# Film factors computed as rows of conditions, bias rows spread in one accumulated product, a new order of pieces: two conditioned attention layers on one core

## The chip, the cores and the metric

The kernel runs on one core of one Trainium2 chip. The metric is the device time of one execution in microseconds (us); lower is better. The core has five engines that run their own instruction streams: TensorE (PE; its weight loads are listed apart as PEld), VectorE (DVE), ScalarE (ACT), GpSimd (POOL) and SyncE (SP), which here only issues DMAs. They wait for each other through semaphores.

## The reference

For 32 sequences of 256 tokens with 256 features, two layers are computed one after the other (masks are all one here, but the kernel handles them):

```python
# layer 0: 8 heads of 32; softmax over features (q) and over time (k)
xn = ln(x, ln_w, ln_b)
q = softmax((xn @ Wq + bq) per head, axis=features)
k = softmax((xn @ Wk + bk + mask) per head, axis=time)
v = (xn @ Wv + bv) * mask
att = einsum('bnhd,bnhl->bhdl', k, v);  y = einsum('bnhd,bhdl->bnhl', q, att)
scale, shift = split(silu(emb) @ W_emb + b_emb)      # emb: 32 x 512, W_emb: 512 x 512
x = x + silu(ln(y) * (1 + scale) + shift) @ W_out + b_out
# layer 1: 16 heads of 16; ordinary attention over 256 tokens, softmax over keys
q, k, v = (xn @ q_w + q_b), (xn @ k_w + k_b), (xn @ v_w + v_b) * mask
y = softmax(q k^T + mask) v;  then the same film, silu and output product as above
```

`silu(emb) @ W_emb` is the film product: it is made once for each layer and for all 32 sequences.

## The kernel before, in words

One "batch" b is one sequence. The work on it is cut into pieces with names: `s0(b)` (statistics of x on VectorE), `r0(b)` (their reciprocal root on GpSimd), `z0(b)` (normalised x, as a high and a low half in f16), `k0`, `q0`, `v0` (projections on TensorE), `km`, `ke`, `kt`, `rk` (softmax of k), `qm`, `qs`, `qe`, `rq` (softmax of q), `att`, `y0`, `Y0(b)` (attention and its division), `s1`, `r1`, `yn0`, `y0T`, `th0`, `st0`, `sh0`, `sl0` (norm, film and silu), `o0`, `x1(b)` (output product and the sum with x: the end of layer 0). Layer 1 has `s2`, `z1`, `q1p`, `k1p`, `v1p`, `qa`, `ka`, `spq`, `spk` (high and low halves of q and k), `rows(b,u)` (scores, for the maximum), `max_(b,u)` on VectorE, `cols(b,u)` (transposed scores), `exp(b,u)` on ScalarE, `pv(b,u)`, `Y1_`, `y1T`, `th1`, `o1` and `o(b)`.

Each engine's stream is a list of such calls written out by hand, in which pieces of some six batches are interleaved, and each piece waits on the semaphores of those that it needs. Where a product lands among the eight PSUM banks is a table, `BANK`, and what must have been read from that bank before is a second table, `FREED`. SP's stream is such a list too: `x_in(b)` loads x, `z0T` and `z1T` transpose by DMA, `wq(b)`/`wk(b)` write the halves of q and k to DRAM and `rq6(b)`/`rk6(b)` read them back in the layout of `rows`.

Ahead of batch 0 stands a setup, whose pieces have no batch number. Weights are loaded (`ld_w1`, `ld_w0`), their largest entries are found and made into powers of two (`w0m`, `w1m`, `mx_w0`, `mx_w1`, `w0p`, `w1p`; TensorE's `tr_*` and `ar_*` carry the maxima across partitions), and each weight is split into f16 halves (`wh_*` on ScalarE at L1739, `wl_*` on VectorE at L1345). Four bias rows are products of a norm's bias with a weight: `row0` to `row3` (L930). To three of them VectorE adds the layer's own bias (`fr0`, `fr1`, `fr2`, L1357), a product with ones spreads the sum over all partitions (`bb0` to `bb2`, L937), and ScalarE copies it out (`bc0` to `bc2`, L1760). Layer 1's q and k biases are needed as columns with the features in another order: ScalarE's `perm` permutes the two biases (L1751) and the two weights (L1754), and `col` multiplies (L990, L991). The film products are `fm0` and `fm1` (L973): for each of four blocks of 128 outputs and each of four blocks of 128 inputs, a 128 x 128 block of the f32 film weight is loaded as the stationary operand and the 32 conditions (`csT`) stream past. `f0m` and `f1m` make the film factors from them on VectorE. `fill_*` (L1775) writes constants into the score operands on ScalarE.

A f32 product stands in the trace as two records, each with its own weight load; a transpose or a f16 product as one.

## Time and profile before

| what | value |
|---|---|
| time before, median of 3 runs | 878.3 us (876.21 to 880.64) |
| profiled execution, its own time | 878.06 us |
| its span, first to last instruction | 876.2 us |
| busy: PE, DVE, POOL, ACT | 827.4, 792.1, 725.7, 708.0 us |

The profiled execution took 878.06 us, of which 1.9 us lie outside the span. Busy time is the time in which at least one instruction of an engine was running. Starts in the rows below are in us from the beginning of the span.

### The profile page before, as it was taken

What the parts mean: (1) busy time and instruction counts of PE and PEld (TensorE: products, weight loads), DVE (VectorE), ACT (ScalarE), POOL (GpSimd) and SP (SyncE); (2) the same over time, 40 slices, a digit from 0 to 9 for tenths busy, and PEclk for the clock granted to TensorE, in tenths of its full rate; (3) what the DMA queues carried; (4) which work ended last, traced back from release to release, by engine and by line L of the source; (5) the groups of instructions that cost most, each with busy time, mean ns of one, the idle gap of its engine ahead of it and who ended that gap; (6) DMA issues with size and microseconds to landing.
All of it is one profiled execution on the core that took longest, in us unless ns stands there. A gap on an engine that the chain in (4) does not pass through costs nothing.

```text
span 876.2 us, 25220 instructions
## 1 busy us (share of the span) xinstructions
PE 827.4 (94%) x8651; PEld 603.3 (69%) x8651; DVE 792.1 (90%) x1633; ACT 708.0 (81%) x1253; POOL 725.7 (83%) x1205
## 2 busy tenths in 40 slices
...
GB/s 230 68 38 33 117 98 92 106 102 109 49 126 133 98 91 115 91 116 110 81 129 57 137 91 102 96 108 116 118 109 89 74 114 91 95 126 113 74 43 37
DMA packets 149306, 85.84 MB, mean 98 GB/s; under 512 B 87478, under 2 KB 141852, under 8 KB 149180
## 3 DMA queue, kind: packets, MB, share of 16 engines
...
## 4 chain that ended last, share of the span: by engine, by line
PE 39%; POOL 19%; DVE 14%; issue 11%; ACT 5%; DMA 0%; SPq 0%; POOLq 0%; DVEq 0%; ACTq 0%
PE banks L688 11%; PE banks L835 7%; DVE NM L1247 4%; PE banks L696 4%; PE banks L822 4%; PE banks L811 4%; POOL ZHL L1928 3%; PE banks L703 3%; POOL Z L1921 3%; DVE st L1148 2%; PE banks L845 2%; POOL YN L1912 2%; POOL SH L1966 2%; POOL ZHL L1925 2%; POOL AB L1994 2%
## 5 line engine op out<-in xcount | busy, mean ns | idle before, releaser
L1247 DVE TENSOR_REDUCE NM<-banks 128x4 f32<-128x1024 f32 x256 | 302.6, 1212 | 12.2 <-PE banks L811 11.6
L1714 ACT ACTIVATE wraw<-banks,uu 128x1024 f32<-128x1024 f32 x154 | 170.2, 1136 | 22.0 <-PE banks L822 21.4
L1714 ACT ACTIVATE PX<-banks,uu 128x1024 f32<-128x1024 f32 x102 | 112.9, 1138 | 11.4 <-PE banks L822 9.9
L688 PE MATMUL banks<-wo,SH 128*128 128x256 f16 x768 | 96.7, 278 | 5.2 <-POOL SH L1966 4.3
L1908 POOL TENSOR_TENSOR rs<-ve,nhalf 128x2 f32<-128x2 f32 x128 | 91.0, 711 | 10.6
L688 PE MATMUL banks<-wv,ZT 128*128 128x256 f16 x768 | 98.6, 280 | 0.9 <-DVE NM L1247 0.8
L811 PE MATMUL banks<-SK,SQ 51*128 51x256 f16 x1024 | 89.3, 273 | 8.0 <-DVE NM L1247 3.9
L1966 POOL TENSOR_TENSOR SH<-ST,SH 128x512 f16<-128x512 f32 x64 | 73.8, 1158 | 26.1 <-ACT SH L1682 26.1
L1696 ACT ACTIVATE R<-banks,fcs,sqs 128x256 f32<-128x256 f32 x128 | 73.5, 574 | 26.7 <-PE banks L696 20.3
L822 PE MATMUL banks<-SQ,SK 53*128 53x256 f16 x1024 | 90.0, 272 | 5.0 <-ACT wemb L1722 1.3
L1928 POOL TENSOR_TENSOR ZHL<-Z,ZHL 128x256 f16<-128x256 f32 x128 | 87.8, 706 | 5.3
L688 PEld LDWEIGHTS banks<-wo,SH 128*128 128x128 f16 x768 | 73.4, 99 | 23.1 <-POOL SH L1966 9.1
L688 PEld LDWEIGHTS banks<-wv,ZT 128*128 128x128 f16 x768 | 74.8, 100 | 17.3 <-issue 7.5
L835 PE MATMUL banks<-wraw,V 128*32 128x256 f32 x1232 | 85.1, 385 | 1.6 <-ACT wraw L1714 0.6
L1994 POOL TENSOR_TENSOR AB<-R,AB 128x512 f16<-128x512 f32 x64 | 74.5, 1166 | 6.0 <-ACT AB L1696 5.7
L1669 ACT ACTIVATE TH<-banks,hB,hA 128x256 f32<-128x256 f32 x128 | 66.2, 580 | 15.7 <-PE banks L703 14.2
L1921 POOL TENSOR_SCALAR Z<-X,nm,rs 128x256 f32<-128x256 f32 x128 | 74.5, 588 | 3.6 <-POOL ZHL L1928 0.5
L1912 POOL TENSOR_SCALAR YN<-Y,nm,rs 128x256 f32<-128x256 f32 x128 | 72.7, 575 | 2.5
L1696 ACT ACTIVATE AB<-banks,fcs,sqs 128x256 f16<-128x256 f32 x128 | 74.0, 578 | 0.0
L811 PEld LDWEIGHTS banks<-SK,SQ 51*128 51x128 f16 x1024 | 39.1, 94 | 47.6 <-issue 25.3
L822 PEld LDWEIGHTS banks<-SQ,SK 53*128 53x128 f16 x1024 | 38.1, 94 | 45.8 <-issue 27.2
L1906 POOL TENSOR_SCALAR nm<-mv 128x2 f32<-128x2 f32 x128 | 29.0, 226 | 49.0 <-DVE mv L1151 48.2
...
## 6 DMA issues: line engine op xcount, KB each, us to landing
...
```

Of the source, the lines that this page charges most:

```text
L688: m = PE.matmul(dst[:, t, :], zt[:, j, k, t * P:(t + 1) * P], w[:, i, k, :], start=(k, n) == (0, 0), stop=(k, n) == (1, 2))
L811: m = PE.matmul(banks[:, n + j % 2, (j // 2) * T:(j // 2) * T + T], SQ[p, r, h, c * P:(c + 1) * P], SK[p, r, h, :], start=True, stop=True)
L822: m = PE.matmul(banks[:, n + j % 2, (j // 2) * T:(j // 2) * T + T], SK[p, r, h, c * P:(c + 1) * P], SQ[p, r, h, :], start=True, stop=True)
L835: m = PE.matmul(banks[32 * j:32 * j + 32, n, 0:T], V1[:, r, c, 4 * g + j, :], px((8 * b + u) % 5)[:, at_px(j):at_px(j) + T], start=(c == 0 ...
L1247: V.tensor_reduce(NMe[:, c, :, 2 * g:2 * g + 2], banks[:, n:n + 2, :].rearrange("p a (h m) -> p a h m", m=T), AX.X, ALU.max, negate=True). ...
L1696: t = A.activation(dst, bank(home(f"g{c}1", b))[:, f, :], ACT.Identity, bias=fcs[:, i, f:f + 1], scale=sqs[:, i:i + 1])
L1714: A.activation(px(v % 5), banks[:, n:n + 2, :].rearrange("p a n -> p (a n)"), ACT.Exp, scale=uu[:, 0:1]).then_inc(S["exp"])
L1908: G.tensor_tensor(rs[:, b % 2, l, :], ve[:, l, :], nhalf[:, :], ALU.pow).then_inc(S[f"r{l}"])
L1921: i = G.tensor_scalar(Z[:, t, :], src[:, t, :], nm[:, b % 2, 2 * l, t:t + 1], rs[:, b % 2, 2 * l, t:t + 1], ALU.add, ALU.mult)
L1928: i = G.tensor_tensor(h[:, 1, k], z[:, :, k, :], h[:, 0, k], ALU.subtract)
L1966: G.tensor_tensor(SH[:, l, 1], ST[:, l], SH[:, l, 0], ALU.subtract).then_inc(S[f"sl{l}"])
L1994: G.tensor_tensor(AB[:, i, :, 1], R1[:, i], AB[:, i, :, 0], ALU.subtract).then_inc(S["sp" + c])
```

## The change

Five things change; the loops, the arithmetic on each batch and all DMA sizes stay.

1. Film: the conditions become the stationary operand (32 columns) and the film weight streams past them, 512 columns at a time (`fx0`, `fx1`, 4 products each). ScalarE copies the 32 x 512 result into the film weight's own tile (`fy0`, `fy1`), and `fm0`/`fm1` are now four transposes of 32 x 128 each.
2. `bb0` to `bb2` take the product with the weight (the norm's bias broadcast over 128 columns) and the layer's bias row in one accumulation; `row0` to `row2` and `fr0` to `fr2` are gone.
3. `rw` makes layer 1's q and k bias rows complete (6 products); `perm` permutes these two rows alone, and `col` is four products of one column.
4. The four copies of weights in `perm` are gone, and with them `xb1(0)`'s wait for `col`.
5. All streams, banks and `FREED` entries are in a new order, SP's too. Counted in pieces, up to `x1(0)` VectorE's list lacks `fr0`, `fr1`, `fr2`, `o1m`, `mx_o1`, `km(3)` and `at_(2)`, and has nothing that stood behind it before.

```diff
-            def bias_all(i):
-                ready(e, f"fr{i}", "cst")
-                clear(e, f"gbb{i}", 0)
-                PE.matmul(at_all(i), ones3[0:1, :], frow[:, i, :], start=True, stop=True).then_inc(C["PE"])
+            def bias_all(i, l, w):
+
+                e.wait_ge(l_w[l], 80)
+                e.wait_ge(l_row, 96)
+                ready(e, "cst")
+                clear(e, f"gbb{i}", 0)
                 for k in range(2):
+                    PE.matmul(at_all(i), lnc[:, l, 1, k:k + 1].to_broadcast([P, P]), wraw[:, 3 * l + w, k, :],
+                              start=(k == 0), stop=False)
+                PE.matmul(at_all(i), ones3[0:1, :], brow[:, i, :], start=False, stop=True).then_inc(C["PE"])
...
-            def film(l):
+            def cond_rows(l):
+
                 ready(e, "csT")
                 e.wait_ge(l_f[l], 64)
+                clear(e, f"gfx{l}", 0)
+                for k in range(4):
+                    t = PE.matmul(at_conds(l), csT[:, k, :], wemb[l][:, k, :], start=(k == 0), stop=(k == 3))
+                t.then_inc(C["PE"])
+
+            def film(l):
+                ready(e, f"fy{l}", "cst")
                 clear(e, f"gfm{l}", 0)
                 for m in range(4):
-                    for k in range(4):
-                        t = PE.matmul(at_film(l, m), wemb[l][:, k, m * P:(m + 1) * P], csT[:, k, :],
-                                      start=(k == 0), stop=(k == 3))
+                    t = PE.transpose(at_film(l, m), wemb[l][0:NB, 0, m * P:(m + 1) * P], ident[0:NB, 0:NB])
                 t.then_inc(C["PE"])
...
+            def rw():
+
+                e.wait_ge(l_w[1], 80)
+                e.wait_ge(l_row, 96)
...
+                for i in range(2):
+                    for k in range(2):
+                        PE.matmul(at_rows(i), lnc[:, 1, 1, k:k + 1], wraw[:, 3 + i, k, :], start=(k == 0), stop=False)
+                    t = PE.matmul(at_rows(i), one1[0:1, 0:1], brow1[:, i, :], start=False, stop=True)
...
-            def bias_sum(i):
-                ready(e, f"row{i}")
-                e.wait_ge(l_row, 96)
-                V.tensor_tensor(frow[:, i, :], at_row(i)[0:1, :], brow[:, i, :], ALU.add).then_inc(C["DVE"])
...
             def perm():
...
-                    for k, e0 in ((0, 0), (0, 1), (1, 0), (1, 1)):
-                        t = A.activation(XB1[:, i, k, e0 * P:(e0 + 1) * P].rearrange("p (f h) -> p f h", f=16),
-                                         wraw[:, 3 + i, k, :].rearrange("p (h e f) -> p e f h", e=2, f=16)[:, e0], ACT.Identity)
...
-            ld_m(); ld_c(); x_in(0); x_in(1); ld_w1(); x_in(2); ld_w0(); mbd0(); ld_r(); ld_f1(); ld_o1(); am(0)
+            ld_m(); ld_c(); x_in(0); x_in(1); ld_w1(); x_in(2); ld_w0(); ld_r(); mbd0(); ld_o0(); ld_f1(); am(0)
```

**TensorE, the setup.** The first place is TensorE's stream from the conditions' transposes to the first projection; each row is an instruction, its output and operands, and how often it follows itself. Before (`row2`, `row1`, ... , the film products, then `k0(0)`):

```order
L964 MATMUL banks<-ident,SQ 128x32 x4
L922 MATMUL banks<-ident,SK 128x32 x4
L930 MATMUL banks<-wraw,lnc 1x256 x4
L865 MATMUL banks<-ident,mxw 3x128
L930 MATMUL banks<-wraw,lnc 1x256 x4
L937 MATMUL banks<-SQ,ones 128x256
L865 MATMUL banks<-ident,mxw 3x128
L937 MATMUL banks<-SQ,ones 128x256
L973 MATMUL banks<-csT,wemb 128x32 x32
L718 MATMUL banks<-ZT,wk 128x256 x6
```

and of the change, from `ar_w0` to the first projections (`rw`, `fx1`, `tr_o0`, `fx0`, `bb0`, `v0(0)`, `v0(1)`, `fm0`, `q0(0)`, `q0(1)`):

```order
L870 MATMUL banks<-mxd,ones 128x3
L995 MATMUL banks<-wraw,lnc 1x256 x2
L996 MATMUL banks<-SK,one 1x256
L995 MATMUL banks<-wraw,lnc 1x256 x2
L996 MATMUL banks<-SK,one 1x256
L965 MATMUL banks<-wemb,csT 32x512 x4
L864 MATMUL banks<-ident,mxw 1x128
L965 MATMUL banks<-wemb,csT 32x512 x4
L939 MATMUL banks<-wraw,lnc 128x256 x2
L941 MATMUL banks<-SK,ones 128x256
L687 MATMUL banks<-wv,ZT 128x256 x24
L972 MATMUL banks<-ident,wemb 128x32 x4
```

The 32 film products with 32 columns became 8 with 512; `row0` to `row2` left, `rw` came, and `v0` and `q0` of batches 0 and 1 now stand ahead of `k0(0)`, with the film transposes between them.

**VectorE, ahead of the first `V`.** The second place is what VectorE does just before the first value tile `v(0)` (L1189 before, L1202 now). Before:

```order
L1345 SCALAR_TENSOR_TENSOR wq<-wraw,sl,wq 128x256 x2
L1148 BN_STATS st<-X 128x6 x2
L1151 BN_AGGR mv<-st 128x2 x2
L1345 SCALAR_TENSOR_TENSOR wk<-wraw,sl,wk 128x128 x4
L1288 TENSOR_REDUCE mxc<-banks 1x1
L1289 TENSOR_SCALAR mxd<-ident,mxc 1x1
L1162 TENSOR_REDUCE km<-banks 128x2
L1163 TENSOR_SCALAR km<-km,un 128x2
L1345 SCALAR_TENSOR_TENSOR wv<-wraw,sl,wv 128x256 x2
L1189 SCALAR_TENSOR_TENSOR V<-banks,un,bbc 128x512
```

and of the change:

```order
L1458 CAST p<-SQ 1x256
L1358 SCALAR_TENSOR_TENSOR wv<-wraw,sl,wv 128x256 x4
L1301 TENSOR_REDUCE mxc<-banks 1x1
L1302 TENSOR_SCALAR mxd<-ident,mxc 1x1
L1358 SCALAR_TENSOR_TENSOR wk<-wraw,sl,wk 128x256 x2
L1358 SCALAR_TENSOR_TENSOR wq<-wraw,sl,wq 128x256 x2
L1202 SCALAR_TENSOR_TENSOR V<-banks,un,bbc 128x512
L1161 BN_STATS st<-X 128x6 x2
L1164 BN_AGGR mv<-st 128x2 x2
```

`s0(3)`, `s0(4)`, `f0m`, `f1m`, `km(0)`, layer 1's `wl_q1` and `wl_k1` and `o1m` moved from ahead of `v(0)` to behind it.

**SP, the first score operands.** The third place is SP's queue around `rk6(0)`, the loads of batch 0's k halves. Before (`wq(0)`, `z1T(1)`, `rq6(0)`, `wk(0)`, `x_in(6)`, `x_in(7)`, `rk6(0)`):

```order
L541 DMA scr<-AB 128x4x256
L521 DMA_TRANSPOSE ZT<-ZHL 128x8x128
L554 DMA SQ<-scr 32x2048
L555 DMA SQ<-scr 16x2048
L554 DMA SQ<-scr 32x2048
L555 DMA SQ<-scr 16x2048
L541 DMA scr<-AB 128x4x256
L514 DMA X<-in_x_dram 128x2x256 x2
L554 DMA SK<-scr 32x2048
```

and of the change (`z1T(0)`, `z0T(5)`, `z1T(1)`, `wq(0)`, `wk(0)`, `mbd1`, `x_in(6)`, `rq6(0)`, `rk6(0)`):

```order
L520 DMA_TRANSPOSE ZT<-ZHL 128x8x128 x3
L540 DMA scr<-AB 128x4x256 x2
L641 DMA mhd<-mh 32x3x256
L513 DMA X<-in_x_dram 128x2x256
L553 DMA SQ<-scr 32x2048
L554 DMA SQ<-scr 16x2048
L553 DMA SQ<-scr 32x2048
L554 DMA SQ<-scr 16x2048
L553 DMA SK<-scr 32x2048
```

`x_in(7)` moved behind `rk6(0)`, and `wq(0)` behind `z1T(1)`. On ScalarE, one `fill` (`fill_q0`) moved from ahead of the `wh_*` to just ahead of `wh_k1` and `ke(0)`.

## Rows read from the trace of the kernel before

**Rows 1.** The page: busy time by engine, share of the span, instructions

```profile
PE 827.4 (94%) x8651; PEld 603.3 (69%) x8651; DVE 792.1 (90%) x1633; ACT 708.0 (81%) x1253; POOL 725.7 (83%) x1205
```

**Rows 2.** Stages: start:end and length, busy (count) of engines, clock, DMA

```profile
10.40:44.40 34.00, 32.52 (x153) 25.15 (x152) 31.63 (x105) 27.87 (x36) 20.40 (x35) 0.70 0.47 129
44.40:70.25 25.85, 25.14 (x210) 21.94 (x209) 23.79 (x67) 11.90 (x28) 16.63 (x27) 0.94 0.16 32
70.25:111.65 41.40, 33.47 (x267) 28.18 (x265) 34.68 (x107) 23.25 (x54) 36.32 (x59) 0.92 0.35 86
150.00:850.00 700.00, 684.51 (x7576) 492.26 (x7572) 652.06 (x1256) 602.41 (x1067) 600.45 (x988) 1.00 0.41 101
```

**Rows 3.** Timeline of VectorE: start, length, instruction

```profile
13.91 0.41 DVE L1357 TENSOR_TENSOR SQ<-banks,SK 1x256 f32<-1x256 f32 x1
...
44.48 0.74 DVE L1189 SCALAR_TENSOR_TENSOR V<-banks,un,bbc 128x512 f32<-128x512 f32 x1
...
70.25 0.74 DVE L1227 SCALAR_TENSOR_TENSOR X<-banks,un,XB 128x512 f32<-128x512 f32 x1
...
111.65 3.48 DVE L1247 TENSOR_REDUCE NM<-banks 128x4 f32<-128x1024 f32 x3
```

**Rows 4.** The same timeline: the work that moves behind `v(0)`

```profile
24.29 1.44 DVE L1345 SCALAR_TENSOR_TENSOR wq<-wraw,sl,wq 128x128 f16<-128x128 f32 x4
...
32.43 0.15 DVE L1383 TENSOR_SCALAR be1c<-bec 128x2 f32<-128x2 f32 x1
...
38.18 0.16 DVE L1399 SCALAR_TENSOR_TENSOR mxw<-bnd 128x1 f32<-128x1 f32 x1
...
39.20 0.74 DVE L1148 BATCH_NORM_STATS2 st<-X 128x6 f32<-128x256 f32 x2
...
40.14 1.72 DVE L1345 SCALAR_TENSOR_TENSOR wk<-wraw,sl,wk 128x128 f16<-128x128 f32 x4
...
42.22 0.67 DVE L1162 TENSOR_REDUCE km<-banks 128x2 f32<-128x512 f32 x1
```

**Rows 5.** Timeline of TensorE (matmuls) in the setup

```profile
15.10 2.79 PE L930 MATMUL banks<-wraw,lnc 128*1 128x256 f32 x8
...
20.05 13.59 PE L973 MATMUL banks<-csT,wemb 128*128 128x32 f32 x64
...
42.39 2.73 PE L688 MATMUL banks<-wq,ZT 128*128 128x256 f16 x12
...
48.84 1.47 PE L688 MATMUL banks<-wq,ZT 128*128 128x256 f16 x12
```

**Rows 6.** TensorE's weight loads around the first change of pace

```profile
16.34 0.13 PEld L930 LDWEIGHTS banks<-wraw,lnc 128*1 128x1 f32 x1 [0.30 <-issue]
16.77 0.13 PEld L930 LDWEIGHTS banks<-wraw,lnc 128*1 128x1 f32 x1 [0.30 <-issue]
17.08 0.30 PEld L930 LDWEIGHTS banks<-wraw,lnc 128*1 128x1 f32 x2 [0.19 <-issue]
```

**Rows 7.** Granted clock (third from the end) by stretches, columns as in Rows 2

```profile
19.00:20.00 1.00, 1.00 (x8) 0.91 (x6) 0.80 (x5) 1.00 (x1) 0.92 (x3) 1.00 0.92 327
...
24.00:28.00 4.00, 4.00 (x21) 4.00 (x20) 3.96 (x8) 4.00 (x12) 2.15 (x2) 0.50 0.03 9
80.00:90.00 10.00, 9.23 (x65) 7.54 (x64) 8.34 (x28) 4.50 (x10) 7.55 (x15) 0.74 0.28 51
```

**Rows 8.** Timeline of ScalarE in the setup

```profile
15.85 5.30 ACT L1775 ACTIVATE SK<-one 32x6144 f16<-32x6144 f32 x1
...
43.18 0.56 ACT L1640 ACTIVATE KE<-banks,km,un 128x256 f32<-128x256 f32 x1 [4.88 <-DVE km L1163]
```

**Rows 9.** SP's queue ahead of the first scores

```profile
99.01 3.12 SPq L514 DMA_DIRECT2D X<-in_x_dram  x2
102.42 0.33 SPq L554 DMA_DIRECT2D SK<-scr  x1
```

**Rows 10.** TensorE's gap between 74 and 79 us, and what ended it

```profile
78.11 0.88 PE L703 MATMUL banks<-ident,KE 128*128 128x128 f32 x4 [3.24 <-ACT KE L1640]
```

More of the change, by code:

```diff
@@ L88 @@
+    "gt_o1": "5",
+    "ga_o1": "2",
+    "gt_f0": "2",
+    "ga_f0": "3",
+    "gt_f1": "0",
+    "ga_f1": "0",
+    "gt_b": "5",
+    "ga_b": "2",
+    "gfx0": "6",
     "gfm0": "1",
+    "gfx1": "1",
     "gfm1": "5",
@@ L258 @@
     "PE": (
-        "cnd pm row2 row1 tr_w1 row0 row3 bb2 tr_w0 bb1 ar_w1 bb0 ar_w0 fm1 fm0 tr_o0 col tr_f0 ar_o0 ar_f0 "
-        "tr_o1 tr_f1 ar_o1 tr_b ar_b ar_f1 ").split(),
+        "pm cnd bb2 tr_w1 row3 tr_w0 ar_w1 bb1 ar_w0 rw fx1 tr_o0 fx0 bb0 fm0 fm1 col tr_f0 ar_o0 ar_f0 tr_b "
+        "tr_o1 ar_b tr_f1 ar_o1 ar_f1 ").split(),
     "DVE": (
-        "mb0 csl csT w1m fr2 fr1 w0m mx_w1 fr0 mc mx_w0 w1p w0p o1m wl_q1 p3 wl_v0 wl_k0 o0m f1m f0m wl_q0 "
-        "wl_k1 mx_o0 wl_v1 mx_f0 o0p film0 mx_o1 wl_o0 bm mx_b o1p mx_f1 fcs mb1 film1 wl_o1 ").split(),
+        "mb0 csl mc csT w1m w0m mx_w1 mx_w0 w1p w0p o0m p3 wl_v1 wl_v0 mx_o0 wl_k0 wl_q0 f0m f1m mx_f0 o0p "
+        "wl_q1 wl_k1 film0 wl_o0 bm mx_b o1m mx_o1 fcs mb1 o1p mx_f1 film1 wl_o1 ").split(),
     "ACT": (
-        "th fill_k1 fill_q0 fill_k0 wh_q1 wh_k1 wh_q0 bc0 wh_v0 wh_k0 perm wh_v1 bc1 fill_q1 wh_o0 bc2 wh_o1 ").split(),
+        "th fill_k0 fill_k1 wh_v0 wh_v1 fy1 wh_q0 wh_q1 wh_k0 fy0 bc1 perm bc0 fill_q0 wh_k1 fill_q1 wh_o0 "
+        "bc2 wh_o1 ").split(),
     "POOL": (
@@ L987, in col @@
                     for f in range(2):
-                        o, cc = at_col(2 * i + f), slice(f * P, (f + 1) * P)
-                        for k in range(2):
-                            PE.matmul(o, XB1[:, i, k, cc], lnc[:, 1, 1, k:k + 1], start=(k == 0), stop=False)
-                        t = PE.matmul(o, prow[:, i, cc], one1[0:1, 0:1], start=False, stop=True)
+                        t = PE.matmul(at_col(2 * i + f), prow[:, i, f * P:(f + 1) * P], one1[0:1, 0:1], start=True, stop=True)
                 t.then_inc(C["PE"])
-            cnd_t(); pm(); row2(); row1(); tr_w1(); row0(); row3(); bb2(); tr_w0(); bb1(); ar_w1(); bb0(); ar_w0()
@@ L1005, in _ @@
-            pv(0, 3); cols(0, 5); k0(8); ty(0, 0); q0(8); v0(8); ktT(8); pv(0, 4); pv(0, 5); rows(2, 2)
-            rows(2, 3); att(7); q1p(4); rows(2, 4); k1p(4); rows(2, 5); rows(2, 6); cols(0, 6); o0(5); cols(0, 7)
+            pm(); cnd_t(); bb2(); tr_w1(); row3(); tr_w0(); ar_w1(); bb1(); ar_w0(); rw(); fx1(); tr_o0(); fx0()
+            bb0(); v0(0); v0(1); fm0(); q0(0); q0(1); fm1(); k0(0); col(); k0(1); ktT(0); tr_f0(); ar_o0(); v0(2)
+            att(0); qtT(0); q0(2); k0(2); k0(3); ktT(1); y0(0); q0(3); qtT(1); att(1); ar_f0(); y0(1); y0T(0)
```

928 lines of the change are left out of this document (460 added, 468 removed), and 214 rows, old and new, of the table FREED.

## The prediction

> **What bounds the kernel now.** I read the busy times first: TensorE 94% of the span, VectorE 90% [rows 1]. Then the stages. From 150 to 850 us TensorE is busy for 684.5 of 700 us and VectorE for 652.1 [rows 2]: two engines are nearly full at once, on work that this change doesn't touch. That part can be reordered but hardly shortened: TensorE's idle time in it, 15.5 us, is the most that another order could win there, while a bad order has no such limit. So an early start pays in full only if nothing later waits longer; and it is the first 111.65 us, up to VectorE's first `max_` [rows 3], that the change rewrites.
>
> In that beginning VectorE is the engine to watch. From 10.4 to 44.4 us it is busy for 31.63 of 34 us, from 44.4 to 70.25 (the first `x1`) for 23.79 of 25.85, and from there to the first `max_` for only 34.68 of 41.4 [rows 2, 3]: first its own queue is the limit, then a chain of latencies. TensorE looks as full in the setup, but 13.59 us of it are the film products [rows 5], and the projections queue behind them. VectorE doesn't wait for this, since its own list, with both films and layer 1's weights ahead of `v(0)`, is just as long: `v(0)` starts at 44.48 [rows 3].
>
> **The clock in the setup.** The weight loads of L930 (256 f32 columns a record) start 0.43 us apart at 16.34 and 16.77, and 0.31 us later comes a row that holds two loads in 0.30 us [rows 6]: the pace doubles at about 17 us, after some microseconds of such products without a gap (8 records from 15.10 on take 2.79 us [rows 5], where 0.43 each would be 3.4). So one record of 256 columns is 0.43 us at 1.2 GHz and 0.21 at 2.4 GHz; the f16 products show the same ratio (12 in 2.73 or 1.47 us, the drain of the last included [rows 5]). Under the film products the granted clock is 0.50, where it was 1.00 at 19 to 20 us [rows 7], and a film record takes 13.59/64 = 0.21 us although only 32 columns stream: the load of 128 f32 columns is what it waits for.
>
> **The change part by part.**
>
> *Film.* 64 records of 0.21 us go. 16 records of 512 columns come. The trace before has no 512-column f32 product; bounded by the nearest, it is between two records of 256 columns at full clock (0.43) and two at half (0.86), so 6.8 to 13.7 us for both layers. At half clock nothing is gained. I take full clock for nearly all of it, because the row with the longest gapless stretch of wide f32 columns, L930, is the one after which the pace doubled, while the film products, with 32 columns between loads, ran at 0.50 throughout [rows 5 to 7].
>
> A page speaks against any gain here: the Trainium skill, "TensorE: Matmul & The Clock Gate", section "LDWEIGHTS (loading the stationary operand)", gives the load's time as its columns divided by 1.2 GHz, whatever the array's clock. By that the 64 loads of the old form would be 6.8 us, as much as the new form's best case, and this term would be zero. The trace disagrees for f32: 0.21 us a record at half clock [rows 5], so the sum goes by the row.
>
> *Bias rows.* `row0` to `row2` and `bb0` to `bb2` become three products of six records each: on TensorE as many wide records as before (12 and 6). What goes is the three adds of VectorE, 0.41 us each (one row stands for the three [rows 3]), 1.2 us of a full queue, and the trip TensorE, VectorE, TensorE. In exchange `bb2` now needs the bias rows at once. VectorE's first add ran at 13.91, so they had landed by then, and they are now issued one DMA earlier. I let TensorE start there at 13.9; before, `row2`, 4 records, needed only the weights and ran ahead of this, so these records move later.
>
> *`rw`, `col`, `perm`.* `rw` adds 12 records of 256 columns (2.6 to 5.1 us), `col` shrinks to four one-column products, and ScalarE loses eight permuting copies. ScalarE isn't the limit: it waited 4.88 us ahead of its first `ke` [rows 8]. It does get one `fill` of 5.3 us [rows 8] between the weights and `ke(0)`, which used to lie in its early idle time. `km(0)` is itself later in VectorE's list than the fill's end, so I cost it at nothing; uncovered it would be 5.3 us on `ke(0)`, though VectorE has `s0(4)`, `f1m` and `q1(1)` to do before it needs ScalarE's results. The 32 x 512 copies and the transposes of 32 rows are in no row; I bound them by zero and the 0.74 us of a 128 x 512 operation, and the waiting engine has other work.
>
> *When TensorE reaches `v0(0)`.* `bb2` (6 records) and `row3` (4) at half clock take 4.3 us from 13.9, to 18.2; the maxima and `bb1` follow, with waits for VectorE, until about 20. Then `rw` 12, `fx1` and `fx0` 16 of double width, `bb0` 6: 50 units of 256 columns. At 0.21 us that ends at 30.7, at 0.43 us at 41.4. `v0(0)` adds 1.3 or 2.7: done at 32.0 or 44.1. A relapse to half clock of some 3 us would cost 1.7.
>
> *When VectorE reaches `v(0)`.* Before: 44.48. Out of its way go `f1m`, `s0(3)` and `f0m` (32.43 to 38.3, 5.8 us), `s0(4)` and `wl_k1` (39.20 to 41.8, 2.6), `wl_q1` 1.4, `km(0)` 0.9, `o1m` 0.7 (as the reduction of 512 columns) and the adds 1.2 [rows 3, 4]: 12.6 us, so it is ready at 31.9. TensorE is done at 32.0 to 33.7; `v(0)` starts at about 33.
>
> *From there to `x1(0)`.* VectorE was busy for 23.8 us between the two [rows 2]. Added is the moved work without the adds, 11.4; gone from ahead of `x1(0)` are `at_(2)`, `km(3)`, `mx_o1` and `o1m`, together 2.7: 32.5 us. Without any idle time `x1(0)` starts at 65.5; with 1.5 us of idle time, where it had 2.1, at 67, 3.3 us before its 70.25.
>
> *From `x1(0)` to the scores.* SP's two loads of x held its queue for 3.12 us from 99.01, and only then, at 102.42, came `rk6(0)` [rows 9]. `x_in(7)`, the one that waits for GpSimd's `xb0(4)`, is now behind it. At most 3.4 us; but `wq(0)` now stands behind `z1T(1)`, and `rq6(0)` waits for that write. I take 1.0 of it. What queued behind `x_in(7)` is only batch 7's load, which has 20 us.
>
> *Sum.* 3.3 + 1.0 = 4.3 us off the profiled execution's span of 876.2, 871.9; with the 1.9 us outside it 873.8. The median of the runs, 878.3, is 0.2 above the profiled execution's 878.06, so the two bases agree.
>
> **The rivals.**
>
> *The lead is swallowed.* From 150 us on the engines work in a fixed order, and any wait for a bank or an SP entry in the new order eats the lead. For it: POOL is busy for 36.3 of the 41.4 us before the first `max_` [rows 2], and its work there is not shorter. Against it: later both full engines have 15.5 and 48 us of slack in 700. Half to all of the lead gone gives 876 to 878.
>
> *The clock stays low (slower than before).* If the wide f32 products are not enough for 2.4 GHz, or the gaps at `tr_w0`, `ar_w1` and `ar_w0` undo it, TensorE ends `v0(0)` at 44.1, VectorE stands idle from 31.9 on, and `x1(0)` comes no sooner than 44.1 + 32.5 = 76.6, 6.4 us late: 883.5 with the 1.0 from SP. It decides from the point at which `v0(0)` ends later than 70.25 - 32.5 = 37.8. Against it stand L930's rows.
>
> *The new order is itself better or worse in the full part.* 15.5 us of TensorE idle time can shrink or double. A third of it either way is 5 us: 869 or 879, and 884 for a bad one.
>
> *The luck of a gap.* Before, TensorE stood 3.24 us for `ktT(4)` [rows 10], and the mean clock of the next 10 us was 0.74 [rows 7], so some 2.6 us of work was lost on a stretch where VectorE also waits. `ktT(4)` now stands further back, behind layer 1's first products. If no such gap opens, the first `max_` is 2 us earlier still: 871.8.
>
> **How the numbers follow.** The forecast (a lead of 2.5 to 9 us that is kept) has 0.50, the last rival inside it; of this 0.43 is beyond 0.5%, 4.4 us, which is about what a measurement of this kernel can tell from no change. The swallowed lead has 0.26, all of it within 0.5%. The low clock has 0.12, slower. The reordered full part has 0.12: 0.04 faster, 0.08 slower. Together faster 0.47, same 0.33, slower 0.20. The predicted time is the likeliest's, 873.8. The range reaches down to 868.5 (`v(0)` at 32.0, no idle time before `x1(0)`, the whole of SP's 3.4 us: 5.7 + 3.4 = 9.1) and up to 882.5, which takes in the swallowed lead and the milder losses of order, and leaves out the low clock and a bad order.
>
> **What would show it.** Right: the 512-column records of `fx1` and `fx0` about 0.43 us apart and granted clock 1.00 over most of 21 to 31 us; `v0(0)` ended by 34; VectorE's first `V` at 33 and first `X` (L1227's successor) at 66 to 68; the first `max_` at 106 to 108; TensorE busy for 97 to 98% from 150 to 845 us. Wrong: 0.86 us between those records; a VectorE gap ahead of `V` or `km`; the first `max_` early and the end not, which puts the loss into the full part.

## The result and the profile after

The changed kernel takes 885.12 us (median of 20 runs, 883.56 to 887.77), the kernel before 879.11 us on the same chip (20 runs, 876.21 to 883.88). The ratio is 1.0065, 95% interval 1.005 to 1.0079: slower, outside the forecast's range. The profiled execution took 884.83 us, 883.0 of them in the span; before, 876.2.

The page's busy times of the changed kernel, which answer to [rows 1]:

```profile
PE 825.6 (94%) x8607; PEld 587.0 (66%) x8607; DVE 795.9 (90%) x1630; ACT 706.4 (80%) x1247; POOL 727.1 (82%) x1205
```

Every engine has about as much work as before, TensorE 1.8 us less, and the span is 6.8 us longer: something waits. The stages, cut at the same events as [rows 2] (the first `V`, the first `X`, the first `max_`):

```profile
10.40:41.31 30.91, 27.73 (x72) 10.29 (x73) 16.66 (x53) 13.81 (x21) 12.74 (x20) 1.00 0.53 135
...
20.40:33.00 12.60, 12.60 (x26) 3.55 (x25) 8.49 (x32) 1.70 (x4) 3.05 (x7) 1.00 0.72 166
...
41.31:76.60 35.29, 28.93 (x235) 24.05 (x233) 32.61 (x106) 24.55 (x38) 23.62 (x41) 0.96 0.13 24
76.60:116.00 39.40, 32.22 (x269) 27.62 (x267) 36.45 (x115) 21.96 (x51) 36.93 (x60) 0.98 0.41 100
150.00:850.00 700.00, 680.41 (x7516) 487.20 (x7514) 660.27 (x1259) 596.71 (x1056) 601.89 (x985) 1.00 0.43 100
```

In the first stage VectorE works for 16.66 of 30.91 us, where it was the full engine before (31.63 of 34). Its timeline names what it waited for:

```profile
34.60 0.28 DVE L1301 TENSOR_REDUCE mxc<-banks 1x1 f32<-1x128 f32 x1 [4.92 <-PE banks L864]
...
38.30 0.88 DVE L1358 SCALAR_TENSOR_TENSOR wk<-wraw,sl,wk 128x256 f16<-128x256 f32 x2 [3.18 <-ACT wk L1738]
...
41.31 0.75 DVE L1202 SCALAR_TENSOR_TENSOR V<-banks,un,bbc 128x512 f32<-128x512 f32 x1 [1.34 <-issue]
...
76.60 0.75 DVE L1240 SCALAR_TENSOR_TENSOR X<-banks,un,XB 128x512 f32<-128x512 f32 x1 [1.52 <-PE banks L687]
...
115.97 1.22 DVE L1260 TENSOR_REDUCE NM<-banks 128x4 f32<-128x1024 f32 x1
```

`v(0)` starts at 41.31, 3.2 us earlier than in [rows 3] but 8 later than forecast, and right behind `v0(0)`, the first 12 of the 24 records at L687, which start at 39.73 and take some 1.4 us. The view puts VectorE's last 1.34 us of idle time down to "issue", which names no other engine; by these times it was TensorE. `x1(0)` starts at 76.60, 6.4 late; the first `max_` at 115.97, 4.3 late; the last `o(31)` at 879.6, 6.8 late (before, 872.8). Both long waits come out of TensorE's queue: `tr_o0` (L864) stands behind `fx1`, and ScalarE's copy `fy1`, which waits for `fx1`, stands ahead of the cast of `wk`. TensorE's timeline (L939 with L941 is `bb2` at 13.58 and `bb1` at 19.62, L929 `row3`, L995 `rw`, L965 `fx1` and then `fx0`, L687 `v0(0)` with `v0(1)`):

```profile
13.58 2.04 PE L939 MATMUL banks<-wraw,lnc 128*128 128x256 f32 x4 [6.13 <-DMA SK<-in_L_cond_k_b_dram]
15.56 1.22 PE L941 MATMUL banks<-SK,ones 1*128 1x256 f32 x2
...
17.01 1.86 PE L929 MATMUL banks<-wraw,lnc 128*1 128x256 f32 x4
...
19.62 2.08 PE L939 MATMUL banks<-wraw,lnc 128*128 128x256 f32 x4
...
23.00 1.86 PE L995 MATMUL banks<-wraw,lnc 128*1 128x256 f32 x4
...
28.46 5.90 PE L965 MATMUL banks<-wemb,csT 128*32 128x512 f32 x8
...
34.49 3.62 PE L965 MATMUL banks<-wemb,csT 128*32 128x512 f32 x8
...
39.73 2.79 PE L687 MATMUL banks<-wv,ZT 128*128 128x256 f16 x24
```

TensorE stands still for 6.13 us until the bias rows are there. From 13.58 on it works without a gap, but at half pace: four records of 256 columns take 1.86 to 2.08 us throughout, and `fx0`, with the same eight records as `fx1`, needs 3.62 where `fx1` needed 5.90. The weight loads inside `fx1` show the change:

```profile
31.87 0.18 PEld L965 LDWEIGHTS banks<-wemb,csT 128*32 128x32 f32 x1 [0.68 <-issue]
32.73 0.18 PEld L965 LDWEIGHTS banks<-wemb,csT 128*32 128x32 f32 x1 [0.68 <-issue]
33.34 0.11 PEld L965 LDWEIGHTS banks<-wemb,csT 128*32 128x32 f32 x1 [0.44 <-issue]
```

0.86 us a record, then less from 33.1 on. So 1.2 GHz until 33.1 us. The clock column of the stage 20.40 to 33.00 says 1.00 all the same: the trace's clock records begin at 33.09, and the view takes a stretch ahead of the first record as full. Ahead of it, only the pace of like instructions tells the clock; "granted clock 1.00 over most of 21 to 31 us", which the forecast named as a sign of being right, can be read off this view and means nothing there.

SP's queue, as in [rows 9], with the first of `rk6(0)` at the second row:

```profile
103.01 0.38 SPq L513 DMA_DIRECT2D X<-in_x_dram  x1
...
105.70 0.30 SPq L553 DMA_DIRECT2D SK<-scr  x1
```

`rk6(0)` comes 29.1 us behind `x1(0)` (before 32.2), and the first `max_` 39.4 us behind it (before 41.4).

### The profile page after: what moved, and what is told of

It is laid out like the page before. It is cut to its first block, busy times and chain, and to the rows that moved or that the text cites. A ratio compares the mean times of both kernels' runs of the same rounds, so it can differ in the third digit from the quotient of the medians.

```text
span 883.0 us, 25115 instructions
## 1 busy us (share of the span) xinstructions
PE 825.6 (94%) x8607; PEld 587.0 (66%) x8607; DVE 795.9 (90%) x1630; ACT 706.4 (80%) x1247; POOL 727.1 (82%) x1205
## 4 chain that ended last, share of the span: by engine, by line
PE 40%; DVE 25%; POOL 15%; issue 12%; ACT 5%; SPq 1%; DMA 1%; POOLq 0%; DVEq 0%; ACTq 0%
PE banks L687 9%; DVE NM L1260 9%; PE banks L834 7%; PE banks L695 5%; PE banks L821 4%; PE banks L810 3%; DVE st L1161 3%; PE banks L702 2%; PE banks L844 2%; POOL ZHL L1934 2%; POOL Z L1927 2%; POOL SH L1972 2%; PE banks L753 2%; DVE ST L1229 1%; POOL XB L1993 1%
## 5 line engine op out<-in xcount | busy, mean ns | idle before, releaser
L687 PE MATMUL banks<-wo,SH 128*128 128x256 f16 x768 | 97.8, 280 | 9.6 <-POOL SH L1972 9.1
L1972 POOL TENSOR_TENSOR SH<-ST,SH 128x512 f16<-128x512 f32 x64 | 73.9, 1163 | 26.8 <-ACT SH L1681 26.7
L687 PE MATMUL banks<-wv,ZT 128*128 128x256 f16 x768 | 94.4, 273 | 1.6 <-DVE X L1240 1.0
L687 PEld LDWEIGHTS banks<-wo,SH 128*128 128x128 f16 x768 | 73.6, 100 | 28.1 <-POOL SH L1972 12.2
L687 PEld LDWEIGHTS banks<-wv,ZT 128*128 128x128 f16 x768 | 72.8, 98 | 15.2 <-issue 7.3
L1918 POOL TENSOR_SCALAR YN<-Y,nm,rs 128x256 f32<-128x256 f32 x128 | 74.7, 590 | 2.8
```

The costliest lines, as they stand in the source:

```text
L687: m = PE.matmul(dst[:, t, :], zt[:, j, k, t * P:(t + 1) * P], w[:, i, k, :], start=(k, n) == (0, 0), stop=(k, n) == (1, 2))
L1972: G.tensor_tensor(SH[:, l, 1], ST[:, l], SH[:, l, 0], ALU.subtract).then_inc(S[f"sl{l}"])
```

## The experiments

Theory L: the loss is TensorE's late `v0(0)`, at 1.2 GHz behind an idle gap. Rivals: the new order of the full part costs it, wherever the start is (O); the content, that is what is computed and how, costs in any order (C); the setup lists of VectorE and ScalarE cost it (Q). Theory M, for the clock itself: it comes up once wide products stand together. All ratios are to the kernel before, run on the same chip.

| kernel | ratio | 95% interval | `v(0)` | `x1(0)` | last `o(31)` |
|---|---|---|---|---|---|
| changed | 1.0065 | 1.005 to 1.0079 | 41.3 | 76.6 | 879.6 |
| + dummies in the gap | 0.9974 | 0.996 to 0.9988 | 32.2 | 66.3 | 868.5 |
| `rw` first | 1.0006 | 0.999 to 1.0022 | 38.9 | 73.0 | 875.0 |
| `rw` first + dummies | 0.9991 | 0.9969 to 1.0012 | 33.8 | 68.0 | 873.2 |
| `row3` ahead of `tr_w1` | 1.007 | 1.0052 to 1.0088 | 42.1 | 76.1 | 878.3 |
| without VectorE's two waits | 1.0071 | 1.0046 to 1.0095 | 41.2 | 76.5 | 879.6 |
| old order, film, transposes late | 1.0093 | 1.0072 to 1.0114 | 50.3 | 76.3 | 877.7 |
| old order, film | 1.0007 | 0.9991 to 1.0022 | 43.8 | 69.5 | 870.3 |
| old order, all, transposes late | 1.0075 | 1.0041 to 1.0109 | 49.4 | 74.9 | 874.5 |
| the same + dummies | 1.0073 | 1.0054 to 1.0092 | 49.6 | 74.3 | 879.5 |
| old order, all | 1.0027 | 0.9997 to 1.0057 | 53.3 | 79.1 | 879.7 |
| old order, all + dummies | 0.9972 | 0.9955 to 0.999 | 43.4 | 68.7 | 870.9 |
| before + dummies | 0.9999 | 0.9977 to 1.002 | 43.9 | 70.7 | 874.9 |

The starts are those of each profiled execution; before, they are 44.5, 70.2 and 872.8.

**Work in the gap.**

```diff
+            def warm(k):
+                for i in range(k):
+                    PE.matmul(banks[0:32, 7, :].rearrange("p (a n) -> p a n", a=4), ident[:, 0:32],
+                              ident[:, :].unsqueeze(1).to_broadcast([P, 4, P]), start=True, stop=True)
...
-            pm(); cnd_t(); bb2(); tr_w1(); row3(); tr_w0(); ar_w1(); bb1(); ar_w0(); rw(); fx1(); tr_o0(); fx0()
+            pm(); cnd_t(); warm(4); bb2(); tr_w1(); row3(); tr_w0(); ar_w1(); bb1(); ar_w0(); rw(); fx1(); tr_o0(); fx0()
```

> The changed kernel with four dummy f32 products of 512 columns added on TensorE between the transposes of the conditions and bb2 (weights and moving data are the identity, the output goes to bank 7, which nobody has used yet), in the 6.1 us in which TensorE otherwise waits for the bias rows. Nothing else moves. Theory L (low clock): the late v0(0) is the price of 1.2 GHz from 13.6 to 33.1 us; then with work in the gap the clock is full well before 28 us, the 8 records of fx1 take about 3.5 us in place of 5.9, v0(0) starts at 31 to 34 in place of 39.7, v(0) at 33 to 37 in place of 41.3, x1(0) at 67 to 71 in place of 76.6, and the time falls by 5 to 8 us against the changed kernel, 0.998 to 1.001 of the kernel before. Theory O (the new order of the full part costs the time, wherever the start is): v0(0) may come earlier, but the ratio stays at 1.005 or above. Mixed: x1(0) as early as before and still 2 to 4 us lost by the end, ratio about 1.003.

Measured: 0.9974. Three weight loads of the dummies, then TensorE and VectorE of this kernel:

```profile
10.78 0.18 PEld L1009 LDWEIGHTS banks<-ident 128*32 128x32 f32 x1 [0.68 <-issue]
11.63 0.12 PEld L1009 LDWEIGHTS banks<-ident 128*32 128x32 f32 x1 [0.68 <-issue]
12.07 0.11 PEld L1009 LDWEIGHTS banks<-ident 128*32 128x32 f32 x1 [0.32 <-issue]
```

```profile
7.36 5.72 PE L1009 MATMUL banks<-ident 128*32 128x512 f32 x8
13.28 1.10 PE L939 MATMUL banks<-wraw,lnc 128*128 128x256 f32 x4 [0.19 <-issue]
...
21.67 3.62 PE L965 MATMUL banks<-wemb,csT 128*32 128x512 f32 x8
...
25.42 3.62 PE L965 MATMUL banks<-wemb,csT 128*32 128x512 f32 x8
```

```profile
32.23 0.75 DVE L1207 SCALAR_TENSOR_TENSOR V<-banks,un,bbc 128x512 f32<-128x512 f32 x1 [1.32 <-issue]
...
66.31 0.75 DVE L1245 SCALAR_TENSOR_TENSOR X<-banks,un,XB 128x512 f32<-128x512 f32 x1 [0.36 <-PE banks L687]
...
105.59 1.22 DVE L1265 TENSOR_REDUCE NM<-banks 128x4 f32<-128x1024 f32 x1
```

The pace doubles at 11.6 us, inside the dummies; the same four records of `bb2` take 1.10 us instead of 2.04, `fx1` 3.62 instead of 5.90. `x1(0)` comes 10.3 us earlier than in the changed kernel, and the last `o(31)` 11.1 earlier: what is won at the start stays, and the work and order of all engines are otherwise the same. So the loss is TensorE at 1.2 GHz, and O can't explain more than a small part. That the idle gap is why the clock stays low, the other half of theory L, is not shown by this: the dummies fill the gap, but they are also products of another shape. `v(0)` waits for TensorE here too: VectorE's `wl_q0` ends at 30.91, and `v0(0)` only starts at 30.66. The expectation of the second run below takes VectorE's list for the limit, which is not so.

**Moving real work into the gap, without and with dummies.** `rw` goes ahead of `bb2`, its products with the bias rows last, its two rows in two banks; `k0(1)` then has to wait for `perm`.

```diff
-        at_rows = lambda i: banks[0:1, home("grw"), i * D:(i + 1) * D]
+        at_rows = lambda i: banks[0:1, (home("grw"), 7)[i], 0:D]
...
-            pm(); cnd_t(); bb2(); tr_w1(); row3(); tr_w0(); ar_w1(); bb1(); ar_w0(); rw(); fx1(); tr_o0(); fx0()
+            pm(); cnd_t(); rw(); bb2(); tr_w1(); row3(); tr_w0(); ar_w1(); bb1(); ar_w0(); fx1(); tr_o0(); fx0()
```

> The changed kernel with rw moved from behind ar_w0 to the front, ahead of bb2: its eight records with layer 1's weights need no bias row and can run from 9.65 us on, where the kernel before ran row2 and row1; only its four records with the bias rows wait for the DMA of 13.5 us. The two rows go to two banks (5 and 7) in place of one, and k0(1) waits for perm. No work is added. Theory L (what was lost is TensorE's time at 1.2 GHz after an idle gap): even if the clock stays at half as long as in the changed kernel, 3.7 us of work have left the stretch behind 13.6 us, so v0(0) starts at about 36 in place of 39.7 and x1(0) at 73, ratio about 1.002; if the work in the gap also brings the clock up, as the dummies did, v0(0) starts at 29 to 31, VectorE is the limit, x1(0) at 66 to 67 and the ratio is 0.996 to 0.999. If neither, above 1.004, the dummies helped for another reason.

> rw at the front and two of the dummy products (four records, 2.9 us) ahead of it, in the 2.4 us in which TensorE waits for layer 1's weights. Theory L: the clock comes up at about 12 us as with the four dummies, and 3.2 us of rw are out of the way behind 13.6 us, so v0(0) could start at 28. VectorE's list is the limit then, it was ready for v(0) at 31.2 with the four dummies: x1(0) at 66 and the ratio 0.996 to 0.999, the same as with the four dummies alone. It would be markedly better only if VectorE's list were not the limit, and it would be at 1.001 or above if the clock stays low again.

TensorE with `rw` first, without dummies:

```profile
9.82 3.57 PE L994 MATMUL banks<-wraw,lnc 128*1 128x256 f32 x8 [2.40 <-DMA lnc<-in_L_cond_norm_b_dram]
14.24 1.86 PE L997 MATMUL banks<-SK,one 1*1 1x256 f32 x4 [0.84 <-DMA SK<-in_L_cond_k_b_dram]
...
25.47 6.46 PE L965 MATMUL banks<-wemb,csT 128*32 128x512 f32 x8
...
37.30 2.79 PE L687 MATMUL banks<-wv,ZT 128*128 128x256 f16 x24
```

In this execution the clock stayed low until 31.2 us, but `v0(0)` starts 2.4 us earlier than in the changed kernel (36 was foreseen), and `x1(0)` is at 73.0, as worked out for this case. The ratio is 1.0006. So the late queue and the low clock both count, and real work in the gap did not bring the clock up in this execution: f32 products ran from 9.82 us on, with one pause of 0.84 us. That speaks against the idle gap as the whole reason. (One of its 12 runs took 874.62 us, 2.9 less than the next; whether its clock came up early is not known.) With two dummies ahead of `rw` the clock rises at 12.5, and then a new gap appears:

```profile
21.60 5.29 PE L965 MATMUL banks<-wemb,csT 128*32 128x512 f32 x8 [1.92 <-DVE iu L1351]
...
27.02 3.62 PE L965 MATMUL banks<-wemb,csT 128*32 128x512 f32 x8
```

```profile
22.80:26.10 3.30, 3.30 (x5) 0.69 (x4) 3.11 (x13) 1.70 (x4) 1.02 (x3) 0.50 1.18 233
```

TensorE is early now, but waits 1.92 us for the bank that VectorE's `w1p` frees, so `fx1` starts at 21.60, where it started at 21.67 with the dummies alone: the work moved ahead wins nothing. At 22.8, 1.2 us after that gap, the granted clock falls to 0.50, `fx1` takes 5.29 us in place of 3.62, and `x1(0)` is 1.7 us later than with the dummies alone. The ratio, 0.9991, is just above what was expected.

**Other neighbours, the same work.**

```diff
-            pm(); cnd_t(); bb2(); tr_w1(); row3(); tr_w0(); ar_w1(); bb1(); ar_w0(); rw(); fx1(); tr_o0(); fx0()
+            pm(); cnd_t(); bb2(); row3(); tr_w1(); tr_w0(); ar_w1(); bb1(); ar_w0(); rw(); fx1(); tr_o0(); fx0()
```

> The changed kernel with row3 and tr_w1 exchanged on TensorE: the four wide records of row3 follow bb2 at once, and the small transpose comes behind both. The work is the same. Theory M (what decides is whether wide products stand together, not how long TensorE has been busy): 10 wide records in a row bring the clock up by some 20 us instead of 33, v0(0) starts at 31 to 34, less the 1.9 us by which tr_w1 and so VectorE's scales are late, x1(0) at 68 to 70, ratio 0.998 to 1.001. If only a busy stretch without a gap counts, or chance of alignment, the exchange changes nothing: v0(0) at about 40, ratio 1.005 to 1.009.

Measured: 1.007. The ten wide records run from 12.41 to 17.3 us without a gap, and the clock still comes up only at 34.5. Theory M falls for this case. `v0(0)` starts at 40.5.

**VectorE's two waits taken away.**

```diff
-            p3_(); wl_v1(); wl_v0(); mx_o0(); wl_k0(); wl_q0(); v(0); s0(3); f0m(); q1(0); v(1); qm(0); km(0)
+            p3_(); wl_v1(); wl_v0(); wl_k0(); wl_q0(); mx_o0(); v(0); s0(3); f0m(); q1(0); v(1); qm(0); km(0)
...
-            th(); fill_k0(); fill_k1(); wh_v0(); wh_v1(); fy1(); wh_q0(); wh_q1(); wh_k0(); fy0(); bc1(); perm()
+            th(); fill_k0(); fill_k1(); wh_v0(); wh_v1(); wh_k0(); wh_q0(); fy1(); wh_q1(); fy0(); bc1(); perm()
```

> The changed kernel with VectorE's two longest waits ahead of v(0) taken away: mx_o0 (4.92 us for tr_o0 behind fx1) goes behind wl_k0 and wl_q0, and ScalarE casts wk and wq of layer 0 ahead of its copy fy1 (3.18 us for wk). TensorE's work and order stay. Theory L: these waits lay under TensorE's late v0(0), so VectorE only waits longer ahead of v(0), which stays at 40.5 to 41.5; x1(0) 75.5 to 76.6 and the ratio 1.004 to 1.008. Rival Q (the new order of VectorE's and ScalarE's setup lists is what costs): x1(0) at 70 or earlier and the ratio below 1.002.

VectorE's waits between 10 and 70 us in this kernel (us in total, times, longest), and its `v(0)`:

```profile
DVE V L1202 <- PE banks L687: 6.2, 1, 6.2
DVE mxc L1301 <- PE banks L864: 6.2, 3, 3.3
```

```profile
41.22 0.75 DVE L1202 SCALAR_TENSOR_TENSOR V<-banks,un,bbc 128x512 f32<-128x512 f32 x1 [6.19 <-PE banks L687]
```

The wait for ScalarE's `wk` is gone and the rest has moved in front of `v(0)` itself: 6.19 us for `v0(0)`, with `v(0)` at the same place to 0.1 us and the ratio at 1.0071. The two waits that the profile of the changed kernel shows most plainly lay under TensorE's delay. Rival Q falls: with these two taken away nothing is won, and with the dummies the changed kernel's own lists give `v(0)` at 32.2.

**The film alone in the old order.**

```diff
-            fm1(); fm0(); k0(0); v0(0); tr_o0(); col(); tr_f0(); q0(0); ar_o0(); v0(1); ar_f0(); tr_o1(); ktT(0)
+            fx1(); fx0(); k0(0); v0(0); fm1(); fm0(); tr_o0(); col(); tr_f0(); q0(0); ar_o0(); v0(1); ar_f0(); tr_o1(); ktT(0)
```

> The kernel before with the film change alone, in its own order: fx1 and fx0 stand where the 64 film products stood, the transposes fm1 and fm0 behind k0(0) and v0(0), and ScalarE's two copies behind wh_k0. Theory L: ahead of these products TensorE starts its setup at 9.65 us as before and is at half clock when it reaches them (24 us); 16 records cost 13.7 us at half clock, what the old form cost, or 6.9 at full. If the clock comes up as long as they run, they take 8 to 11 us, v0(0) is done earlier than before, VectorE's v(0) stays at 44.5 because VectorE's own list is as long, and the ratio is 0.997 to 1.002. If the content of this edit were itself the loss (transposes and ScalarE's copies as a chain), film0 and with it th0(0) would be late and the ratio above 1.004.

Measured: 1.0093, a miss of my own making. Its TensorE, and VectorE's longest wait:

```profile
33.14 1.04 PE L723 MATMUL banks<-ZT,wk 128*128 128x256 f16 x6 [4.56 <-DMA augs<-p]
```

```profile
DVE be1c L1400 <- PE banks L985: 6.1, 1, 6.1
```

The transposes stood behind `k0(0)`, which waits 4.56 us for the DMA of `augs`, and VectorE's `f1m` waited for them. With them directly behind `fx0`:

```diff
-            fx1(); fx0(); k0(0); v0(0); fm1(); fm0(); tr_o0(); col(); tr_f0(); q0(0); ar_o0(); v0(1); ar_f0(); tr_o1(); ktT(0)
+            fx1(); fx0(); fm1(); fm0(); k0(0); v0(0); tr_o0(); col(); tr_f0(); q0(0); ar_o0(); v0(1); ar_f0(); tr_o1(); ktT(0)
```

> The film change alone in the old order once more, mended where the first try was slow by its own doing: there the transposes stood behind k0(0), which waits 4.6 us for the DMA of augs, and VectorE waited 6.1 us for them ahead of f1m. Now fm1 and fm0 follow fx0 at once. Nothing else differs from the kernel before than the film products and the two copies on ScalarE. Theory: fx1 and fx0 take 8.8 us as there, the transposes end at about 29.8, VectorE reaches f1m at 32.1 and does not wait, v(0) at 44 to 45, x1(0) at 69.5 to 71, ratio 0.998 to 1.002. If the film change itself costs, VectorE waits ahead of be1c again and the ratio is above 1.004.

Measured: 1.0007, `v(0)` at 43.8 and `x1(0)` at 69.5. Two short groups of transposes on the wrong side of one waiting product had cost 6.8 us at `x1(0)`. Put right, the film change costs and gives nothing in the old order.

**The whole change in the old order.** First with the transposes late, without and with four dummies (`warm(4)` behind `pm()`), then in the right place (`fm1(); fm0();` directly behind `fx0();`). The diffs of the first to the kernel before, TensorE's and ScalarE's and VectorE's lists; the functions are those of the change:

```diff
-            cnd_t(); pm(); row2(); row1(); tr_w1(); row0(); row3(); bb2(); tr_w0(); bb1(); ar_w1(); bb0(); ar_w0()
-            fm1(); fm0(); k0(0); v0(0); tr_o0(); col(); tr_f0(); q0(0); ar_o0(); v0(1); ar_f0(); tr_o1(); ktT(0)
+            cnd_t(); pm(); tr_w1(); row3(); bb2(); tr_w0(); bb1(); ar_w1(); bb0(); ar_w0()
+            rw(); fx1(); fx0(); k0(0); v0(0); fm1(); fm0(); tr_o0(); col(); tr_f0(); q0(0); ar_o0(); v0(1); ar_f0(); tr_o1(); ktT(0)
...
-            mb0(); csl_(); s0(0); s0(1); csT_(); s0(2); w1m(); fr2(); fr1(); w0m(); mx_w1(); fr0(); mc(); mx_w0()
+            mb0(); csl_(); s0(0); s0(1); csT_(); s0(2); w1m(); w0m(); mx_w1(); mc(); mx_w0()
...
-            th(); fill_k1(); fill_q0(); fill_k0(); wh_q1(); wh_k1(); wh_q0(); bc0(); wh_v0(); wh_k0(); perm()
+            th(); fill_k1(); fill_q0(); fill_k0(); wh_q1(); wh_k1(); wh_q0(); bc0(); wh_v0(); wh_k0(); fy1(); fy0(); perm()
```

> The content of the whole change (film past the conditions, three bias products, q and k biases of layer 1 as rows, no adds on VectorE) in the order of the kernel before on all engines, with its banks. What is left out is the new order alone. TensorE's first wide product still waits for the bias rows or for tr_w1, till 12 to 14 us. Theory L: clock at half till some 30 us, k0(0) and v0(0) end at 40 to 44; VectorE has its old long list, ready for v(0) at 43.3 (44.5 less the adds), so x1(0) at 69.5 to 71.5 and the ratio 0.998 to 1.002, well below the changed kernel. Theory C (the content is what costs, in any order): x1(0) later than 74, ratio above 1.004.

> The same as the content in the old order, with the four dummy products of 512 columns (identity by identity, into bank 7, which rw uses later) on TensorE behind its first transposes. Theory L: the clock comes up before fx1, k0(0) and v0(0) end by 35, VectorE never waits for them, x1(0) at 68.5 to 69.5, ratio 0.996 to 0.999, at most 1 us better than without the dummies, because in this order VectorE's own list is the limit. If it is slower than without them, dummy work in front costs more than the clock gives.

> The whole change in the old order, mended in the same way: fm1 and fm0 directly behind fx0. Theory: without the waits for the transposes x1(0) starts at 68.5 to 70.5 (VectorE's list is shorter by the three adds only), ratio 0.997 to 1.001. Then the content of the change costs nothing wherever it is placed, and gains nothing in the old order; all of the loss is in where the new order put it. If it stays above 1.004, the content costs.

The first two repeat the wait for the transposes (`v(0)` at 49.4 and 49.6) and say little on the content. The first one's 12 runs fall into two groups, six of 879.68 to 880.42 us and six of 884.81 to 892.11. With the dummies its 6 runs took 881.74 to 885.17, so there they did not bring the times down to the lower group: in the profiled executions `x1(0)` came 0.6 us earlier than without them, the last `o(31)` 5.0 later. The granted clock was up at 12.9 but fell to 0.50 again at 33.4 and at 40.2; where the 5 us were lost is open. Of the third, half of 12 runs took 874.47 to 879.23 us and half 883.74 to 888.42; its profiled execution is of the upper half. The first one's profiled execution, of its lower group, shows the other side. TensorE in the first and in the third (L932 `row3`, L942 and L944 `bb2`):

```profile
14.34 1.87 PE L932 MATMUL banks<-wraw,lnc 128*1 128x256 f32 x4
16.14 2.06 PE L942 MATMUL banks<-wraw,lnc 128*128 128x256 f32 x4
18.13 0.69 PE L944 MATMUL banks<-SK,ones 1*128 1x256 f32 x2
...
25.31 7.05 PE L968 MATMUL banks<-wemb,csT 128*32 128x512 f32 x16
```

```profile
14.34 1.86 PE L932 MATMUL banks<-wraw,lnc 128*1 128x256 f32 x4
16.13 2.08 PE L942 MATMUL banks<-wraw,lnc 128*128 128x256 f32 x4
18.14 1.22 PE L944 MATMUL banks<-SK,ones 1*128 1x256 f32 x2
...
31.51 9.36 PE L968 MATMUL banks<-wemb,csT 128*32 128x512 f32 x16
```

The two kernels differ only in the place of the transposes, which is behind `fx0` in both. Up to the start of L944 the two streams are the same instructions at the same times, to 0.01 us. Then one runs at full clock from 18.1 us on, the other at half until 36.2. In the second the film products (L968) end at 40.9, the transposes behind them, and VectorE waits:

```profile
41.26 0.17 DVE L1394 TENSOR_SCALAR be1c<-bec 128x2 f32<-128x2 f32 x1 [5.07 <-PE banks L975]
```

That puts `v(0)` at 53.3 and `x1(0)` at 79.1, 8.9 us later than in the kernel before. With the dummies in front and the transposes right:

> The whole change in the old order (transposes directly behind fx0) with the four dummy products. Without them the times of this kernel fell into two groups, 874.5 to 879.2 and 883.7 to 888.4 us, and of its near twin the profiled execution had its clock up at 18.05 us, while its own had it up at 36.18, with the same products at the same times until then. Theory P: the groups are executions in which the chip raised the clock early or late; then with the dummies only the first group is left, all runs at 873 to 880 us, ratio 0.996 to 1.000, x1(0) at 68 to 70. If both groups are still there, they have another cause.

Measured: 0.9972, and the upper group is gone, all 12 runs are between 874.83 and 879.16 us. So the two groups are most likely executions whose clock comes up early or late; only one execution of each kernel was profiled, so this is not shown run by run. Rival C, as it was put, falls: with the clock up the content costs nothing in the old order and is worth 1.6 us at `x1(0)` (68.7). But with the clock late it does cost, in the old order too, the 8.9 us above. What the change brought in is a chain that hangs on the clock, `rw` and the film products ahead of transposes that VectorE waits for; in the new order it ends in `v0(0)`.

**Control: dummies in the kernel before.** 

```diff
-            cnd_t(); pm(); row2(); row1(); tr_w1(); row0(); row3(); bb2(); tr_w0(); bb1(); ar_w1(); bb0(); ar_w0()
+            cnd_t(); pm(); warm(2); row2(); row1(); tr_w1(); row0(); row3(); bb2(); tr_w0(); bb1(); ar_w1(); bb0(); ar_w0()
```

> The kernel before with two dummy products (four records, 2.9 us) on TensorE ahead of row2: the control for the dummies. Its granted clock was at half from 20.4 to 37.4 us too, but VectorE's own list held v(0) at 44.5. Theory L: fm1 and fm0 may go a little faster, v(0) stays within 0.7 us of 44.5, the ratio is 0.998 to 1.002, so that what the dummies give the changed kernel is not something that they give any kernel. If the ratio is below 0.997, dummies help by themselves and the changed kernel's lead over the kernel before is theirs.

Measured: 0.9999, `v(0)` at 43.9. Dummies by themselves give nothing that can be measured; there VectorE's own list is the limit. The control is not one of the kernel before at full clock: the clock was up at 12.0 but granted at 0.50 again from 18.8 to 35.9, and the 64 film records took 13.86 us, against 13.59 in [rows 5].

## Why the prediction was wrong

**The step that failed** is one sentence: "I take full clock for nearly all of it". With it fell "At 0.21 us that ends at 30.7": the queue from `bb2` to `v0(0)` ran at half clock until 33.1, `v0(0)` began at 39.7, and `v(0)` at 41.3, 8 us after its forecast. The rival "the clock stays low" is what came, at a chance of 0.12. Its point of decision, `v0(0)` later than 37.8, was passed by 3 us or so, and its figures came out, 76.6 for `x1(0)` to the tenth and a span of 881.6 against 883.0. The tenth is luck of two errors: TensorE was done 3 us before the 44.1, since the clock did rise inside `fx1` (though `rw` began at 23.0, where the sum has about 20), and the way from `v(0)` to `x1(0)` was 35.3 instead of 32.5.

**Why the chance was too small.** I rested the clock on L930's rows of one execution. They show a rise inside the last eight of sixteen such records, at about 17 us, in a kernel that had begun them at 9.65. The prediction moved those records ("these records move later") and priced only the move. It did not ask what the 6.13 us of idle time left in their place may do to the clock, though [rows 7] shows it at 0.50 through other f32 products, the films. That this idle time is what kept it low stays unproven: with `rw` in the gap it was low until 31.2 as well. And a clock shown for one execution was taken as a property of the kernel; the two equal streams above, with the clock up at 18.1 and at 36.2 us, show that it can be one of the execution. The Trainium skill, "TensorE: Matmul & The Clock Gate", Part 1, section "What's actually happening", says that the hardware's watch over activity runs freely, so the same kernel shows different numbers of slow products from run to run. The two streams agree that the moment varies, but the page has it vary by 500 ns either way, and here it is 18.1 us; no run here shows that the watch's phase is the reason.

**The other steps can be read off the kernel with four dummies**, which is the change with the clock that I had assumed:

- 512-column records: forecast 0.43 at full clock and 0.86 at half; measured 0.45 (3.62/8) and 0.86.
- VectorE ready at 31.9, `v(0)` at about 33: measured 30.9 and 32.2.
- From `v(0)` to `x1(0)` 32.5 and 1.5 idle: measured 34.1. `x1(0)` at 67: measured 66.3.
- SP's order 1.0: from `x1(0)` to the first `max_` 39.3 us, 2.1 less than before, twice the term. `rk6(0)` came 29.2 us behind `x1(0)`, 2.9 sooner than before. How much of the 2.1 is SP's order and how much the gap of [rows 10], which did not open here (TensorE's longest from 66 to 100 us is 1.94), was not separated.
- First `max_` at 106 to 108: measured 105.6, 6.1 earlier than before.
- ScalarE's `fill`, copies and transposes at nothing: ScalarE still waited for `km(0)` ahead of `ke(0)`, 1.48 us here and 1.50 in the changed kernel. Right.
- Span 871.9: measured 871.9. This is partly luck: of the lead of 6.1 us at the first `max_`, 4.3 were left at the last `o(31)`.
- The range's low end, 868.5, is a slip: its terms give 878.1 - 9.1 = 869.0. Nothing hangs on it.

**The new order of the full part** gives back some 2 us: 6.1 less 4.3 with the dummies; in the changed kernel, 4.3 late at the first `max_` and 6.8 at the end. TensorE's idle time from 150 to 850 us is 19.6 us (15.5 before), 18.5 with the dummies. This is a mild form of the third rival. "The lead is swallowed" by half or more didn't come: there was no lead, and where there was one, about two thirds were kept. "The luck of a gap": one opened in the changed kernel as well, 3.43 us ahead of `o0`, at 73.9.

**Open.** Why the clock stays low from 13.6 us on in every profiled execution of this order and its variants without dummies (up at 33.1, 31.2, 34.5 and 33.0 us; the changed kernel's 20 runs lie within 4.2 us and show no second group), while the old order with all of the change had it up at 18.1 in one execution and, by the times, perhaps in half of its runs. Whether the dummies help because they fill the gap or by their shape (512 columns past 32 stationary ones) was not tested. Putting wide products together didn't settle it, and a mended bank for `fx1` with `rw` first was not tried. The versions that beat both kernels are the changed kernel with four dummies, 0.9974, and the whole change in the old order, transposes right, with four, 0.9972; they can't be told apart.
